# The first mixture of experts routed in blocks of 64 slots instead of run densely, and a reordered front in the last mixture

## The chip, the cores and the metric

One core of a Trainium2 chip runs the whole program. The metric is the device time of one execution in microseconds (us). Engines: TensorE (PE; its weight loads are PEld), VectorE (DVE), ScalarE (ACT), GpSimd (POOL) and SyncE (SP), which issues most DMAs. Each engine runs its own instruction list in order, and semaphores order the engines among each other.

## The reference, cut to what matters

A two-layer perceiver block on 512 tokens (8 sequences of 64) of width 256. The change touches the feed-forward part of layer 0, behind its small attention, and a little of the feed-forward part of layer 1:

```python
# layer 0: every token, the two best of 8 experts, hidden width 512
probs = softmax(mla_out @ router_w + router_b)
topw, topi = top_k(probs, 2)
topw = topw / (topw.sum(-1, keepdims=True) + 1e-08)
combine = sum(one_hot(topi, 8) * topw[..., None], axis=-2)
h1 = gelu(einsum('bsd,edf->ebsf', mla_out, w1) + b1)
h2 = einsum('ebsf,efd->ebsd', h1, w2) + b2
return hs + 0.3 * einsum('bse,ebsd->bsd', combine, h2)
# layer 1: the same with the one best of 8 experts, hidden width 1024, silu
```

The reference multiplies every token by every expert and weighs with `combine`, which is zero for six of the eight.

## The kernel before, in words

The program is a row of stages, each a block that all engines enter and leave together (the branch that ends a block is named by its line; "PEq" as a releaser is this barrier). `core.x` (in the trace: resid) is the residual, 512 tokens as 4 tiles of 128 x 256. PSUM has eight banks of 128 x 512 fp32.

**Layer 0's mixture, `Mixture` with `Gate` and `Experts` (tiles d_*).** It is dense. Its input is c_mlaT (128 x 2 x 512, features on partitions), which ACT writes at the end of the attention block in `ffn0`. TensorE computes router logits (L966), DVE the softmax, ranks and weights (L929 to L952). For each of 8 experts TensorE then computes 4 hidden chunks of 128 features for all 512 tokens (`first`) and 4 x 4 output tiles (`second`). Each product of two fp32 matrices is made as three fp32r matmuls of a high and a low part (`product3`, L186). ACT and POOL split the weights into these parts (L1068, L1041), ACT applies Gelu (L1084) and splits h (L1088), DVE takes its low part (L1107) and adds each expert's output, times the token's weight, to x (L1115). Expert loops are `each`: first and last iteration written out, a hardware loop between. b2 is added once for all experts by the matmul of transposed weights (L1194). Four of the weight splits (`experts.high`, `gpsimd_first`) stand in the attention block ahead, on ACT (L1068 at 259 to 271 us) and POOL.

**Layer 1's mixture, `Routed` (tiles k_*).** It is routed already, with one choice a token. 8 + 7 = 15 blocks of 64 slots hold the tokens sorted by expert; a pair of blocks fills 128 slots. The order of the work on each engine is written out by hand. TensorE counts the tokens before each one (L2640), DVE turns this into a slot number a token (L2542 to L2553), then a 0/1 matrix (`gather_map`, L2570) with which TensorE gathers 256 slots a time (`gather`, L2663) into PSUM, and DVE copies them to k_xg (`gathered`, L2560). Groups 0 and 1 of slots are gathered so; groups 2 and 3 come by device memory: POOL scatters the normalised rows with an indirect DMA (L2466), reads them back in slot order (L2470), and TensorE transposes them (`gather_rows`, L2673). A pair's step is `hidden` (L2689: fp32, 64 slots a matmul, the two blocks of a pair in the two 64-column halves of the array), activation, `turn` (L2701), a copy of the transposed h on ACT (L2498), and `output` (L2718). Results of pairs below VIA go to device memory (L2474) and come back by token with four indirect DMAs (L2479); the last two pairs go back through matmuls with 0/1 matrices (`scatter`, L2728). Experts of blocks 8 to 14 depend on the data: SP reads their numbers from k_expert (`value_load`, L2449) and loads their weights. `warm` (L96) is a run of matmuls whose result nobody reads. TensorE adds b2 ahead of the first gather (L2653), and DVE writes `gather_map(1)` ahead of `gathered(0)`.

## Time and profile before

| | us |
|---|---|
| three executions | 1010.16, 1007.88, 1010.75; median 1010.16 |
| the profiled execution | 1008.23 |
| its span, first to last instruction | 1006.5 |
| mean granted TensorE clock | 0.984 |
| TensorE matmuls busy | 962.3 (96%) |
| weight loads / DVE / ACT / POOL busy | 798.6 / 552.5 / 498.2 / 180.8 |

Times of rows are us from the span's start. A timeline row gives start, duration, engine, line, operation, output<-input, the count of merged instructions, and in brackets how long the engine sat idle before it and what released it. One fp32 matmul shows as two records, a transpose or fp32r matmul as one.

### The profile page before, as it was taken

Reading aid. Unit: us, or ns where it says so; the run is one execution under the profiler, and the core shown is the slowest. Engines: PE = TensorE matmul, PEld = TensorE weight load, DVE = VectorE, ACT = ScalarE, POOL = GpSimd, SP = SyncE. Lnnn points to the kernel's source line nnn. Section 1 sums busy time; section 2 is a strip of 40 time slices with the busy share of each in tenths; the row PEclk is TensorE's granted clock in tenths of the full one; section 3 lists DMA queues with packets and bytes.
Section 4 is the critical chain, followed back from the end, with each engine's and each line's share of the span. In section 5 each row is a group of like instructions: output and inputs, shape, how many; then the busy total and the mean of one; then the engine's idle time right before and its main releaser. Section 6 shows DMA issues by size and latency. Waiting matters only on the chain. (4 is left out here: it accounts for less than half of the span.)

```text
span 1006.5 us, 20977 instructions
## 1 busy us (share of the span) xinstructions
PE 962.3 (96%) x8756; PEld 798.6 (79%) x8756; DVE 552.5 (55%) x800; ACT 498.2 (49%) x716; POOL 180.8 (18%) x188
## 2 busy tenths in 40 slices
PE   8999999888899999899999999999999999998997
PEld 7888887665689985689999999998989996656554
DVE  5677777666443354655646465656464642367222
ACT  5777776353666645454444454454444532321332
POOL 2000000022224423022221222222222101420101
PEclk9999999899999999999999999999999999997999
DMA  5111110022022304111111111111113000599895
GB/s 172 69 47 48 47 49 3 3 62 65 12 81 89 93 20 167 43 42 43 43 43 42 42 42 42 42 42 42 42 62 136 0 1 1 138 327 306 283 346 185
DMA packets 57365, 84.55 MB, mean 84 GB/s; under 512 B 5505, under 2 KB 46162, under 8 KB 57298
## 3 DMA queue, kind: packets, MB, share of 16 engines
q1 hardware_dynamic: 56466, 81.22, 25.6%
q0 software_dynamic: 832, 2.36, 0.7%
q8 instruction: 52, 0.85, 0.3%
q14 instruction: 15, 0.12, 0.0%
HBM read 80.94 MB, written 2.62 MB: 83 GB/s over the span
## 5 line engine op out<-in xcount | busy, mean ns | idle before, releaser
L186 PE MATMUL ps<-f_pT_hi,f_cN_hi 128*128 128x256 f32 x512 | 145.4, 284 | 0.0
L186 PE MATMUL ps<-f_pT_hi,f_cN_lo 128*128 128x256 f32 x512 | 144.7, 283 | 0.0
L186 PE MATMUL ps<-f_pT_lo,f_cN_hi 128*128 128x256 f32 x512 | 144.7, 283 | 0.0
L1596 ACT ACTIVATE e_pr<-ps,e_negmax 128x1024 f32<-128x1024 f32 x64 | 71.5, 1117 | 129.9 <-DVE e_negmax L1601 127.6
L1870 DVE TENSOR_TENSOR f_pT_lo<-ps,f_pT_hi 128x1024 fp32r<-128x1024 f32 x64 | 78.3, 1224 | 81.8 <-ACT f_pT_hi L1808 81.7
L186 PE MATMUL ps<-e_cT_hi,e_qb_hi 128*128 128x512 f32 (+1 forms) x288 | 115.3, 400 | 0.0
L186 PE MATMUL ps<-e_cT_hi,e_qb_lo 128*128 128x512 f32 (+1 forms) x288 | 109.8, 381 | 0.0
L186 PE MATMUL ps<-e_cT_lo,e_qb_hi 128*128 128x512 f32 (+1 forms) x288 | 109.1, 379 | 0.0
L1808 ACT CAST f_pT_hi<-ps 128x1024 fp32r<-128x1024 f32 x64 | 64.9, 1014 | 84.6 <-PE ps L1920 83.8
L445 DVE SCALAR_TENSOR_TENSOR a_u<-ps,a_floor,a_cap 128x1024 f32<-128x1024 f32 x64 | 79.2, 1279 | 48.2 <-PE ps L540 47.7
L186 PEld LDWEIGHTS ps<-f_pT_hi,f_cN_hi 128*128 128x128 f32 x512 | 97.8, 191 | 2.6 <-issue 0.8
L186 PEld LDWEIGHTS ps<-f_pT_lo,f_cN_hi 128*128 128x128 f32 x512 | 97.9, 191 | 1.7
L186 PEld LDWEIGHTS ps<-f_pT_hi,f_cN_lo 128*128 128x128 f32 x512 | 97.9, 191 | 0.0
L356 ACT ACTIVATE a_pr<-a_u,a_nb 128x1024 f32<-128x1024 f32 x64 | 73.8, 1152 | 43.7 <-DVE a_u L445 42.4
L1601 DVE TENSOR_REDUCE e_negmax<-ps 128x1 f32<-128x1024 f32 x64 | 78.1, 1221 | 31.0 <-PE ps L186 30.7
L1591 POOL TENSOR_TENSOR e_cT_lo<-e_raw,e_cT_hi 128x512 fp32r<-128x512 f32 x32 | 40.3, 1292 | 160.7 <-ACT e_cT_hi L1790 160.7
L1920 PE MATMUL ps<-ident,e_pr 128*128 128x128 f32 x512 | 66.3, 272 | 2.5 <-PEq L1625 1.2
L1774 POOL TENSOR_TENSOR f_cN_lo<-e_raw,f_cN_hi 128x512 fp32r<-128x512 f32 x32 | 40.3, 1286 | 141.4 <-ACT f_cN_hi L1797 141.4
L186 PEld LDWEIGHTS ps<-e_cT_hi,e_qb_hi 128*128 128x128 f32 x288 | 54.5, 189 | 11.4 <-issue 1.8
L186 PEld LDWEIGHTS ps<-e_cT_hi,e_qb_lo 128*128 128x128 f32 x288 | 54.3, 188 | 11.2
L1920 PEld LDWEIGHTS ps<-ident,e_pr 128*128 128x128 f32 x512 | 57.8, 140 | 5.5 <-issue 2.8
L186 PEld LDWEIGHTS ps<-e_cT_lo,e_qb_hi 128*128 128x128 f32 x288 | 54.7, 190 | 8.5
(401 smaller groups left out, 1961.8 us busy)
## 6 DMA issues: line engine op xcount, KB each, us to landing
k_w<-in_L_ffn_W SPq DMA_DIRECT2D x30, 1024.0 KB, 13.5
a_ctxT<-in_ctxT SPq DMA_DIRECT2D x16, 512.0 KB, 4.4
d_w<-in_L_ffn_w SPq DMA_DIRECT2D x32, 256.0 KB, 2.7
e_raw<-in_ctxT SPq DMA_DIRECT2D x8, 1024.0 KB, 4.9
e_raw<-in_ctx SPq DMA_DIRECT2D x8, 1024.0 KB, 5.5
k_b<-in_L_ffn_b SPq DMA_DIRECT2D x14, 256.0 KB, 12.0
k_w<-in_L_xattn_w_q SPq DMA_DIRECT2D x1, 1024.0 KB, 5.0
e_wk<-in_L_xattn_w_k SPq DMA_DIRECT2D x1, 1024.0 KB, 7.5
```

What stands on the lines that cost most here:

```text
L186: last = nc.tensor.matmul(out, a[i], b[j], start=start and n == 0, stop=stop and n == 2, skip_group_check=skip)
L356: A.activation(pr[:, n % NP, :], u[:, n % NU, :], ACT.Square, bias=nb[:], scale=HD ** -0.5).then_inc(p_ready, 1)
L445: V.scalar_tensor_tensor(u[:, n % NU, :].rearrange("p (r w) -> p r w", r=RT), core.psum[:, 0:2048].rearrange("p (r w) -> p r w", r=RT)[:, ...
L1591: nc.gpsimd.tensor_tensor(cT[1][:, c, cols], rawT[:, c, cols], cT[0][:, c, cols].bitcast(F32), ALU.subtract).then_inc(t_lo, 1)
L1596: nc.scalar.activation(pr[:, p % NPR, :], core.ps[p % 2][:], ACT.Exp, bias=negmax[:, p:p + 1], accum_out=total[:, p:p + 1]).then_inc(exp_r ...
L1601: nc.vector.tensor_reduce(negmax[:, p:p + 1], core.ps[p % 2][:], AX, ALU.max, negate=True).then_inc(max_ready, 1)
L1774: nc.gpsimd.tensor_tensor(cN[1][:, ks, :], raw[:, ks, :], cN[0][:, ks, :].bitcast(F32), ALU.subtract).then_inc(n_lo, 1)
L1808: nc.scalar.copy(pT[0][:, g, :, P * (p % 2):P * (p % 2) + P], core.ps[2][:].rearrange("p (k n) -> p k n", n=P)).then_inc(pT_hi, 1)
L1870: nc.vector.tensor_tensor(pT[1][:, g, :, cols], core.ps[2][:].rearrange("p (k n) -> p k n", n=P), pT[0][:, g, :, cols].bitcast(F32), ALU.s ...
L1920: last = nc.tensor.transpose(core.ps[2][:, k * P:(k + 1) * P], pr[:, p % NPR, k * P:(k + 1) * P], core.ident[:])
```

## The change

**Layer 0's mixture.** `Gate`, `Experts` and `Mixture` go; `Paired` takes their place. Two choices a token make 1024 places in 8 + 15 = 23 blocks of 64 slots, that is 12 pairs in 6 groups of 256 slots. Products are plain fp32, nothing is split except the gather's input. The weights of blocks 0 to 7 (1 MB an expert) are all loaded in the attention block ahead, into 8 of 14 ring places; those of the 15 data-dependent blocks follow in the mixture. Groups 0 to 2 are gathered by matmul, 3 to 5 by device memory; pairs 0 to 8 return by device memory, in two gathers a token tile, and pairs 9 to 11 by fp32 matmuls with a matrix that holds the token's weight. The four weight splits in the attention block go, on ACT and POOL alike. Two DMAs fill the unused rows with zeros.

```diff
+class Paired:
+    RING = 14
+    BS = 64
+    TOP = 2
+    LAST = 3
+    ROWS_FROM = 3
...
+        self.EXTRA = (self.TOP * NT - 1) // self.BS
+        self.NB = E + self.EXTRA
+        self.NP = (self.NB + 1) // 2
+        self.NG = self.NP // 2
...
+    def prepare_sync(self, sp):
...
+        for e in range(E):
+            self.load(sp, e, e)
+        sp.wait_ge(self.zeroed, 1)
+        for rows, first in ((self.x_rows, 2 * P * self.ROWS_FROM), (self.y_rows, P * (self.NP - self.LAST))):
+            n = self.NP - first // P
+            sp.dma_start(rows[first:, :].rearrange("(i p) d -> p i d", p=P), bc(self.zero[:], 1, n)
+                         ).then_inc(self.zero_out, 16)
...
+            @block.sync
+            def _(sp):
+                sp.wait_ge(expert_ready, 1)
+                for i in range(EXTRA):
+                    k = E + i
+                    if k >= RING:
+                        sp.wait_ge(y_psum, (k - RING) // 2 + 1)
+                    self.load(sp, k, sp.value_load(expert[0:1, i:i + 1], min_val=0, max_val=E - 1))
+            @block.gpsimd
+            def _(pool):
...
+                for i in range(2):
+                    for j in range(TT):
+                        g.indirect_dma_start(self.x_rows, rows(i, j), mrows[:, j, :], None).then_inc(x_put, 16)
+                pool.wait_ge(x_put, 16 * 2 * TT)
+                for i in range(NG - RF):
...
+                for n in range(VIA):
+                    pool.wait_ge(y_copied, n + 1)
+                    g.dma_start(self.y_rows[P * n:P * n + P, :], whole[n % 2][:]).then_inc(y_out[n % 2], 16)
+                pool.wait_ge(y_out[0], 16 * ((VIA + 1) // 2))
+                pool.wait_ge(y_out[1], 16 * (VIA // 2))
+                for j in range(TT):
+                    for i in range(2):
+                        g.indirect_dma_start(back[i][:, j, :], None, self.y_rows, rows(i, j)).then_inc(y_back[j], 16)
+            @block.scalar
+            def _(act):
...
+                for i in range(4):
+                    rows(i)
+                for q in range(NG):
+                    if q >= 1:
+                        taken(2 * q - 2)
+                        taken(2 * q - 1)
+                    if 2 * (2 * q + 1) + 1 >= E and not chosen:
+                        act.wait_ge(expert_ready, 1)
+                        chosen += [act.value_load(expert[0:1, i:i + 1], min_val=0, max_val=E - 1) for i in range(EXTRA)]
+                    turned(2 * q)
+                    turned(2 * q + 1)
+                taken(NP - 2)
+                taken(NP - 1)
...
+                for q in range(NG):
+                    if q >= 1:
+                        hidden(2 * q)
+                        output(2 * q - 2)
+                        hidden(2 * q + 1)
+                        output(2 * q - 1)
+                    turn(2 * q)
+                    turn(2 * q + 1)
+                    if 2 * q - 1 >= VIA:
+                        scatter(2 * q - 1)
+                    if q + 1 < NG:
+                        (gather if q + 1 < RF else gather_rows)(q + 1)
+                output(NP - 2)
+                scatter(NP - 2)
+                output(NP - 1)
+                scatter(NP - 1)
```

`turned(n)` is eight Gelu activations of 128 x 64 (four feature chunks, two blocks of a pair, each with its expert's bias); `taken(n)` copies a pair's output out of PSUM; `scatter_map` and `spread` build the weighted matrices.

**Layer 1's mixture.** The b2 matmuls move behind the last `output`, eight more warming matmuls stand at their old place, and `gathered(0)` moves ahead of `gather_map(1)`.

```diff
+                gathered(0)
                 gather_map(1)
-                gathered(0)
...
-                core.warm(2, 1)
-                pe.wait_ge(mineT_ready, 1)
-                pe.wait_ge(self.b_in, 16)
-                for j in range(TT):
-                    t.matmul(acc(j), mineT[:, j * P:(j + 1) * P], self.b2[:], start=j % 2 == 0, stop=False,
-                             skip_group_check=True)
+                core.warm(2, 9)
...
                 for n in steps(NP - 1):
                     output(n)
+                pe.wait_ge(mineT_ready, 1)
+                pe.wait_ge(self.b_in, 16)
+                for j in range(TT):
+                    t.matmul(acc(j), mineT[:, j * P:(j + 1) * P], self.b2[:], start=False, stop=False,
+                             skip_group_check=True)
                 scatter(NP - 1)
```

**The order of instructions.** First, ACT in the new mixture, from the table load of the first `turned` on; d_hT rows are the Gelu activations, d_whole rows are `taken`, and L1104 is the `value_load` line:

```order
169 L1082 ACT_TABLE_LOAD
170 L1082 ACTIVATE d_hT<-ps,d_b 128x64 x16
171 L1094 COPY d_whole<-ps 128x256 x2
172 L1082 ACTIVATE d_hT<-ps,d_b 128x64 x16
173 L1094 COPY d_whole<-ps 128x256 x2
174 L1104 TENSOR_LOAD d_expert
175 L1104 ISA x2
176 L1104 TENSOR_LOAD d_expert
177 L1104 ISA x2
```

Fifteen such TENSOR_LOADs with their two register instructions stand between `taken(3)` and the activations of pair 4. The dense mixture had none on any engine.

Second, TensorE in the new mixture around the join of two rounds (L1303 hidden, L1324 output, L1314 turn, L1281 gather_rows; the rows are consecutive from the last output matmuls of pair 3 on):

```order
828 L1324 MATMUL ps<-d_w_6,d_hT 64x256
829 L1324 MATMUL ps<-d_w_7,d_hT 64x256
830 L1314 MATMUL ps<-ident,d_h 128x128 x8
831 L1281 MATMUL ps<-ident,d_xr 128x128 x4
832 L1303 MATMUL ps<-d_w_12,d_xg 64x512
833 L1303 MATMUL ps<-d_w_13,d_xg 64x512
834 L1303 MATMUL ps<-d_w_12,d_xg 64x512
835 L1303 MATMUL ps<-d_w_13,d_xg 64x512
836 L1324 MATMUL ps<-d_w_8,d_hT 64x256
837 L1324 MATMUL ps<-d_w_9,d_hT 64x256
```

The gather of a group stands directly ahead of the hidden layer that reads it, and only one hidden layer stands between the transposes of pair 4 and its output.

Third, the end of the program on TensorE, before:

```order
2310 L2718 MATMUL ps<-k_w_6,k_hT 64x256 x8
2311 L2728 MATMUL ps<-k_y_hi,k_permT 128x256
2312 L2728 MATMUL ps<-k_y_lo,k_permT 128x256
2313 L2728 MATMUL ps<-k_y_hi,k_permT 128x256
2314 L2728 MATMUL ps<-k_y_lo,k_permT 128x256
```

and now:

```order
2288 L2827 MATMUL ps<-k_w_6,k_hT 64x256 x8
2289 L2867 MATMUL ps<-k_b,k_mineT 128x256 x4
2290 L2837 MATMUL ps<-k_y_hi,k_permT 128x256
2291 L2837 MATMUL ps<-k_y_lo,k_permT 128x256
2292 L2837 MATMUL ps<-k_y_hi,k_permT 128x256
```

The four b2 matmuls now stand between the last output and the last scatter.

## Rows read from the trace of the kernel before

**Rows 1.** The page: busy time of each engine.

```profile
PE 962.3 (96%) x8756; PEld 798.6 (79%) x8756; DVE 552.5 (55%) x800; ACT 498.2 (49%) x716; POOL 180.8 (18%) x188
```

**Rows 2.** Windows: us, busy (count) PE, PEld, DVE, ACT, POOL, PE clock, DMA share, GB/s.

```profile
274.00:278.00 4.00, 3.17 (x16) 3.10 (x16) 1.51 (x3) 1.11 (x2) 0.00 (x0) 0.60 0.54 162
...
283.00:373.00 90.00, 89.33 (x570) 80.43 (x569) 36.23 (x62) 57.88 (x93) 36.16 (x28) 1.00 0.24 70
...
917.00:919.00 2.00, 2.00 (x11) 1.88 (x10) 1.14 (x4) 0.00 (x0) 0.00 (x0) 0.50 0.99 260
...
925.00:933.00 8.00, 8.00 (x28) 6.55 (x28) 5.72 (x29) 0.26 (x1) 3.20 (x4) 0.50 1.08 315
...
934.00:999.60 65.60, 64.94 (x454) 35.84 (x452) 13.75 (x21) 22.02 (x39) 8.70 (x12) 1.00 0.88 289
```

**Rows 3.** Timeline, where layer 0's mixture begins.

```profile
271.93 0.38 ACT L1361 ACTIVATE c_aoT<-ps,c_bv 128x128 f32<-128x128 f32 x1
...
274.37 3.17 PE L966 MATMUL ps<-d_gate_w,c_mlaT 128*128 128x8 f32 x16 [0.82 <-PEq L1275]
...
278.35 0.23 ACT L959 ACTIVATE d_gate_p<-d_gate_p 128x32 f32<-128x32 f32 x1 [2.96 <-DVE d_gate_p L931]
...
281.11 0.42 DVE L944 TENSOR_REDUCE d_gate_rank<-d_gate_gt 128x32 f32<-128x256 f32 x1
```

**Rows 4.** Timeline, where it ends and the next block begins.

```profile
375.31 0.74 DVE L1142 BATCH_NORM_STATS2 stats<-resid 128x6 f32<-128x256 f32 x2
...
376.59 2.25 PE L96 MATMUL ps<-ident 128*128 128x128 f32 x18 [1.53 <-PEq L1224]
```

**Rows 5.** Timeline, two pairs' steps in layer 1's mixture.

```profile
964.19 1.09 PE L2701 MATMUL ps<-ident,k_h 128*128 128x128 f32 x8
...
972.25 1.09 PE L2701 MATMUL ps<-ident,k_h 128*128 128x128 f32 x8
...
973.18 0.60 PE L2673 MATMUL ps<-ident,k_xr 128*128 128x128 f32 x4
...
973.71 3.65 PE L2689 MATMUL ps<-k_w,k_xg 128*64 128x512 f32 x16
```

**Rows 6.** Timeline, the front of layer 1's mixture.

```profile
924.17 0.22 DVE L2542 TENSOR_TENSOR k_more<-ps,k_steps 128x56 f32<-128x56 f32 x1 [0.70 <-PE ps L2643]
...
925.31 3.78 PE L2653 MATMUL ps<-k_b,k_mineT 8*128 8x256 f32 x8
...
926.58 1.14 DVE L2570 TENSOR_SCALAR k_perm<-k_slots,k_slot 128x256 fp32r<-128x256 f32 x4
927.63 0.86 DVE L2575 TENSOR_SCALAR k_diag<-ident,k_slot 128x128 f32<-128x128 f32 x4
...
929.02 0.58 PE L2663 MATMUL ps<-k_perm,k_x_hi 128*128 128x256 f32 x1
...
932.60 1.51 PE L2737 MATMUL ps<-k_diag,k_ones 128*128 128x128 f32 x8
932.84 0.69 DVE L2560 COPY k_xg<-ps 128x512 f32<-128x512 f32 x1 [1.83 <-PE ps L2663]
```

**Rows 7.** One line, SP's value_load: duration ns min/median/max, first and last start.

```profile
L2449 SPq TENSOR_LOAD <-k_expert x7: 263/442/482, 929.2 to 933.2; - x7
L2449 SPq FUSED_REGOPS  x7: 147/147/173, 929.7 to 933.7; - x7
```

**Rows 8.** Timeline, the end of the program.

```profile
989.59 0.54 POOL L2474 DMA_DIRECT2D k_y_rows<-xnT  x1 [7.52 <-ACT xnT L2505]
...
994.76 1.02 POOL L2479 DMA_INDIRECT xn<-k_y_rows,k_place  x1 [4.63 <-issue]
...
998.61 0.95 POOL L2479 DMA_INDIRECT xn<-k_y_rows,k_place  x1 [0.30 <-issue]
...
1000.61 0.36 PE L2728 MATMUL ps<-k_y_hi,k_permT 128*128 128x256 f32 x1 [1.02 <-DVE k_y_lo L2604]
```

**Rows 9.** One line, ACT's weight splits: columns as in rows 7.

```profile
L1068 ACT CAST d_w_hi<-d_w x32: 609/618/625, 259.3 to 363.0; 128x512 fp32r<-128x512 f32 x32
```

More of the change, by code:

```diff
@@ L1201 @@
[L1201 to L1224 removed]
+                        pattern=[[1, P]], channel_multiplier=-1).then_inc(self.const, 1)
@@ new lines, in _ @@
+                for i in range(2):
+                    step(V.reduce_sum(wts[i][:], pick[i][:], AX), i == 1)
+                for i, values in enumerate((slot[0], slot[1], wts[0], wts[1])):
+                    spread(i, values)
+                gather_map(1)
+                for q in range(NG):
+                    copied(2 * q)
+                    copied(2 * q + 1)
+                    if q + 1 < NG:
+                        gathered(q + 1)
+                    if q + 2 < RF:
+                        gather_map(q + 2)
+                    if q == 2:
+                        dve.wait_ge(row_ready, 4)
+                        for n in range(VIA, NP):
+                            scatter_map(n)
@@ new lines, in scatter @@
+                def scatter(n):
+                    pe.wait_ge(map_ready, n - VIA + 1)
+                    pe.wait_ge(y_copied, n + 1)
+                    for j in range(TT):
+                        last = t.matmul(acc(j), back_to[n - VIA][:, j * P:(j + 1) * P], whole[n % 2][:],
+                                        start=False, stop=n == NP - 1, skip_group_check=True)
+                    last.then_inc(placed, 1)
+                pe.wait_ge(m_lo, 1)
+                gather(0)
+                hidden(0)
@@ new lines, in _ @@
+                hidden(1)
+                pe.wait_ge(weighed, 1)
+                for j in range(TT):
+                    last = t.transpose(y_bank[0:E, j * P:(j + 1) * P], wt[:, j, :], core.ident[:])
+                last.then_inc(wT_psum, 1)
+                for i in range(4):
+                    spread(i)
+                pe.wait_ge(wT_ready, 1)
+                pe.wait_ge(self.b_in, 32)
+                for j in range(TT):
+                    t.matmul(acc(j), wT[:, j * P:(j + 1) * P], self.b2[:], start=j % 2 == 0, stop=False,
+                             skip_group_check=True)
@@ L1528, in _ @@
                 output(1)
-        mixture.run(mlaT, None, finished)
+        mixture.run(mlaT)
 def xattn1(core, a, finished, early):
```

623 lines of the change are left out of this document (332 added, 291 removed).

## The prediction

> **What bounds the kernel now.** I read the page first: TensorE's matmuls are busy for 96% of the span [rows 1], so before each stage's waits are looked at, its TensorE time counts. The windows then show the stage that changes: from 283 to 373 us TensorE is busy for 89.33 of 90.00 us at clock 1.00 (the 2.4 GHz level), while DVE, ACT and POOL have slack [rows 2]. The dense mixture is bound by matmuls alone. The timeline gives its ends: router logits start at 274.37 us [rows 3], the next block's first matmul at 376.59 us [rows 4]. So the stage takes 102.2 us, and this is what the routed version must beat. I count from L, the start of the logits.
>
> Layer 1's mixture is the model for the new one, since the instructions have the same shapes. One step there (hidden, output, turn) for a half pair takes 4.03 us: the transposes of two pairs start at 964.19 and 972.25 us with two steps between [rows 5]. In 65.6 us it makes 15 such steps at clock 1.00 [rows 2].
>
> **The change part by part.** What goes is some 90 us of full TensorE work. What comes is 12 pair steps of 4.03 us, 48.4 us, as each pair of 64-slot blocks has one 512-wide hidden chunk. Three matmul gathers add about 2.0 us each at the full level (the one of 929.02 to 932.60 us took 3.6 us at clock 0.50 [rows 2, 6]), three `gather_rows` 0.60 us each [rows 5], three scatters 1.7 us each (four 256-column fp32 matmuls of 0.43 us: 512 columns for each block pair take 3.65/8 = 0.46 us in two concurrent halves [rows 5], twice that alone). All this is 61 us. The rest is waits, since work is now in short pieces that pass from engine to engine.
>
> *Front, L to L+19.4.* Logits 3.2 us [rows 3]; eight transposes at the half level, L+5.1; ACT then makes two copies of about 1.05 us, L+7.3, and DVE the low part, 1.2 us, plus waits, L+9.0. Ranks are ready sooner (281.5 us, L+7.2 [rows 3]), so the warming matmuls ahead of the counts are not late. DVE's slot chain took 2.4 us in layer 1 (924.17 to 926.58 us [rows 6]); it is longer by some two-choice operations, 2.8 us: L+11.9. `gather_map(0)` is 4 operations as before (1.14 us [rows 6]) and 4 with two inputs of about 0.45 us: 3.0 us, L+14.9. TensorE has then waited some 3 us, and I take the gather at the half level, as in layer 1, 3.6 us; the copy to d_xg with its hand-overs (932.60 to 933.5 us there, 0.9 us [rows 6]) ends at L+19.4.
>
> *To the first `turn`, L+37.5.* `hidden(0)` and `hidden(1)`: 3.65 us at the full level [rows 5], 1.5 us more for the part at the half level, L+24.6. Weight transposes, 0.6 us. Then four `spread`s follow each other: DVE's four diagonals (0.86 us), TensorE's eight records (1.51 us at clock 0.5, half of that else) [rows 6], ACT's copy beside DVE. I take 2.35 us a turn, L+34.6, with the level falling meanwhile. `gather_map(1)` stands behind the last diagonals on DVE and ahead of `copied(0)`, which `turn(0)` waits for: 3.0 us and two copies of 0.7 us give L+37.5. The b2 matmuls (3.78 us at the half level [rows 6]) run beside this.
>
> *Rounds.* Two turns and `gather(1)` partly at the half level, 4.1 us, copy 0.9 us: L+42.5. A round is 8.06 us plus its gather, and since the gather stands right ahead of `hidden` the 0.9 us copy is waited for in each: in layer 1 another hidden layer hid it. Round 1 takes 11.0 us (L+53.5), round 2, whose gather is the short one, 9.6 us (L+63.1). One `turned` is eight activations. A 32-column one without a bias row takes 0.23 us, a 128-column one with bias 0.38 us [rows 3]; between them, less overlap, I take 0.27 us each, 2.2 us, and it fits under `gather` and `hidden`.
>
> *The fifteen loads.* In round 2 ACT reads 15 expert numbers right after `taken(3)`, which ends about L+60.6. No ACT row shows such a load. The nearest are SP's seven: starts from 929.2 to 933.2 us, 0.67 us apart, made of 0.44 us for the load and 0.15 us for its register operation [rows 7]. Fifteen are 10.0 us; with the shortest load (0.26 us) and almost nothing else the lower bound is 4.8 us, and with the longest ones and gaps the upper 11 us. I take 10.0: L+70.6, activations 2.2 us, L+72.9. TensorE could go on at L+64.9 (`hidden(6)` done), so it stands for 8.0 us. After such a pause it starts at 1.2 GHz. In layer 1's front the 8.0 us from 925 us ran at clock 0.50 without a gap before the level rose [rows 2]; I charge 7 us at half speed, 3.5 us lost. Without the pause both terms go. The Trainium skill, DMA: Bandwidth & Descriptors, section "Latency and other measured facts", puts a `tensor_load` floor at about 600 ns and says that the compiler unrolls four times "to amortize". The trace disagrees on the floor: its median is 442 ns [rows 7]. By the page's floor with SP's register time the fifteen would cost 11.5 us; what its amortizing would give is the first rival below.
>
> *To the end.* The rest of round 3 is 9.7 us with the lost time, its gather 1.5 us: L+84.1; round 4, L+93.7. In round 5 pair 8 is out of PSUM 4.2 us later, L+97.9. Its rows must be in memory before the gathers back: from POOL's last write to its first indirect gather 5.2 us passed [rows 8]. Then eight gathers of 1.28 us follow on POOL (four from 994.76 to 998.61 us started that far apart [rows 8]), where layer 1 has four: L+113.3. Landing 1.7 us (estimate from the end of that trace), two additions 0.95 us, then four additions of the matmul part and four statistics, 3.2 us, barrier 0.5 us: L+119.7. TensorE's own path (three scatters between the last outputs) would be done at L+111.7, so POOL's gathers end the stage. The stage is 17.5 us longer than 102.2.
>
> *Around it.* In the attention block ahead four ACT splits of 0.62 us go [rows 9], which stood between exponentials and copies: gain between 0 and 2.5 us, I take 1.1. The 8 MB of early weights flow while TensorE runs small tiles; the mixture's last six ring places and nine reloads have 20 us or more of slack each at 289 GB/s [rows 2], so nothing is charged. Behind the stage TensorE has now stood still before the barrier; after such a gap the stretch from 917 us ran at 0.50 [rows 2]: 1.4 us lost, between 0 and 3.
>
> *Layer 1's front.* Nine warming matmuls at the half level take 9 x 0.43 = 3.8 us, as long as one and the b2 matmuls of 3.78 us [rows 6] less 0.5 us, so the gather starts 0.5 us sooner; `gathered(0)` waits for TensorE in either order. At the end b2 takes 2 us at the full level where 1.02 us was idle [rows 8]. I take zero, between 1.2 us gained and 0.6 us lost.
>
> The sum: 17.5 - 1.1 + 1.4 + 0 = 17.8 us on the profiled execution's 1008.23 us, **1026 us**. That execution is 1.9 us below the median of the runs shown, which widens the range a little and moves nothing else. About 0.3% is what a measurement of this kernel can tell from no change.
>
> **Rivals.**
> *The loads are amortized* or run beside ACT's waits. For it: only a register is written, and SP's first load took 0.26 us. Against: each of SP's seven was followed by its register operation at an even pace [rows 7]. Below about 1.7 us for all fifteen TensorE hardly waits; the 8.0 us pause shrinks to 0 or 1 and its 3.5 us go: 1015 us. This is the page's amortizing carried out. By spreads and tail at their better ends, 1008.
>
> *The waits hide, not slower.* TensorE's work decides, as before the change: front to L+19.4, then 12 steps, gathers, scatters and spreads back to back, about 65 us, and 4 us behind them, L+88.6, 13.6 us shorter: 995 us. It takes TensorE work between `hidden(1)` and `turn(0)`, under each copy and under the loads. It decides from the point where less than some 13 us of the waits remain; I count about 30. Against it stands the written order, which leaves nothing to run in those places.
>
> *The half level stays.* TensorE works in pieces of 2 to 8 us with gaps of 0.9 us; if the level does not rise again in rounds 3 and 4, two rounds cost 8 us more each in the worst case, about 10 together: 1036 us. Against: layer 1's steps hold 1.00 [rows 2], though with fewer gaps.
>
> **How the numbers follow.** Forecast 0.55, loads amortized 0.22, waits hidden 0.10, half level 0.13. The forecast's own range is 1017 to 1034: loads 5.2 us less, spreads and tail 2 to 4 us either way, around it 2 us. Ten per cent below go with hidden waits and the best amortized cases; some below the top with the last rival: 1010 to 1037. Faster by over 0.3%: 0.08, nearly all from hidden waits. Within 0.3%: 0.10, from the better half of the amortized case. Slower: 0.82.
>
> **What would show it.** Right: 15 loads in ACT's queue at 0.6 to 0.7 us, TensorE idle before `output(4)` for about 8 us with a clock near 0.5 behind it; about 37 us from logits to `turn(0)`; POOL's eight indirect gathers as the last thing that DVE waits for; rounds of 9.6 us. Wrong: loads below 0.3 us, TensorE at 1.00 through the stage, spreads that overlap with `hidden`, a weight that TensorE waits for, or a stage of under 100 us.

## The result, and the profile after

| | before | after |
|---|---|---|
| median of the runs, us | 1010.45 (1007.88 to 1012.66) | 1024.72 (1020.29 to 1029.0) |
| the profiled execution, its span | 1008.23, 1006.5 | 1029.0, 1027.3 |
| mean granted clock | 0.984 | 0.972 |
| TensorE busy | 962.3 | 955.7 |
| layer 0's mixture, logits to the next block | 102.2 | 117.4 |

The ratio is 1.0147, 95% interval [1.0118, 1.0175]: slower, near the forecast of 1026.0. TensorE is busy for 6.6 us less in all (in the new mixture for 90.1 us where the dense one had 99.1) and yet the span is 20.8 us longer. From the starts of four stages, the difference of the spans splits as follows: up to layer 0's logits -0.3 us, the new mixture +15.2, all between it and layer 1's logits +1.8, from there to the end +4.1. That sums to 20.8.

First the page of the changed kernel, to be held against [rows 1]:

```profile
span 1027.3 us, 20845 instructions
PE 955.7 (93%) x8718; PEld 769.4 (75%) x8718; DVE 554.0 (54%) x837; ACT 467.1 (45%) x733; POOL 165.0 (16%) x195
```

TensorE in the new mixture, from the timeline of the changed kernel (the first and last rows answer to the logits of [rows 3] and to the next block of [rows 4]). L1303 is `hidden`, L1290 `spread`, L1349 b2, L1314 `turn`, L1324 `output`, L1332 `scatter`:

```profile
274.06 1.92 PE L1244 MATMUL ps<-d_gate_w,c_mlaT 128*128 128x8 f32 x16 [0.82 <-PEq L1389]
290.55 5.67 PE L1303 MATMUL ps<-d_w,d_xg 128*64 128x512 f32 x16 [0.79 <-DVE d_xg L1169]
296.58 1.06 PE L1290 MATMUL ps<-d_diag,d_ones 128*128 128x128 f32 x8
299.07 1.16 PE L1290 MATMUL ps<-d_diag,d_ones 128*128 128x128 f32 x8 [1.43 <-issue]
303.34 2.08 PE L1290 MATMUL ps<-d_diag,d_ones 128*128 128x128 f32 x8 [3.11 <-DVE d_diag L1181]
...
312.09 1.97 PE L1314 MATMUL ps<-ident,d_h 128*128 128x128 f32 x8
317.26 1.94 PE L1303 MATMUL ps<-d_w,d_xg 128*64 128x512 f32 x8 [0.78 <-DVE d_xg L1169]
...
337.44 1.94 PE L1303 MATMUL ps<-d_w,d_xg 128*64 128x512 f32 x8 [0.78 <-DVE d_xg L1169]
345.78 3.64 PE L1324 MATMUL ps<-d_w,d_hT 128*64 128x256 f32 x16 [6.40 <-ACT d_hT L1082]
355.11 1.94 PE L1303 MATMUL ps<-d_w,d_xg 128*64 128x512 f32 x8 [0.78 <-DVE d_xg L1169]
...
372.43 1.89 PE L1332 MATMUL ps<-d_whole,d_map 128*128 128x256 f32 x8
380.16 3.56 PE L1332 MATMUL ps<-d_whole,d_map 128*128 128x256 f32 x8 [3.96 <-issue]
391.50 2.25 PE L96 MATMUL ps<-ident 128*128 128x128 f32 x18 [2.27 <-PEq L975]
```

The brackets are the waits. I cut the stage in three: the **front** from the logits to `hidden(2)` (317.26), 43.2 us; the **rounds** to the first `scatter` (372.43), 55.2 us; the **tail** to the next block, 19.1 us. These three numbers are the yardstick for every experiment below.

The same stage in windows, with the granted clock before the DMA share (compare [rows 2], where TensorE was busy without a gap at 1.00):

```profile
core 0: us, PE busy (x) PEld busy (x) DVE busy (x) ACT busy (x) POOL busy (x), PEclk, DMA share, GB/s
290.00:293.00 3.00, 2.45 (x6) 0.77 (x8) 2.72 (x16) 0.00 (x0) 1.75 (x2) 0.50 0.94 317
...
317.00:337.00 20.00, 18.61 (x132) 10.81 (x132) 6.60 (x15) 4.89 (x20) 2.22 (x4) 1.00 0.72 250
337.00:345.00 8.00, 1.94 (x8) 0.48 (x8) 7.21 (x11) 1.02 (x6) 0.00 (x0) 0.84 1.07 371
345.00:349.00 4.00, 3.22 (x16) 1.89 (x18) 0.00 (x0) 2.37 (x12) 0.00 (x0) 0.50 0.72 244
349.00:372.00 23.00, 21.43 (x153) 11.42 (x150) 4.84 (x7) 9.02 (x38) 3.62 (x6) 0.99 0.21 76
```

In the rounds TensorE is busy for 93% of its time at the full level, except in one hole of 6.4 us, behind which the level is 0.50 for 4 us. The hole is ScalarE's: between its copy of pair 3 and pair 4's Gelu activations, with nothing but the 15 register loads (ScalarE's queue at their line, columns as in [rows 7]: shortest, median and longest ns):

```profile
L1104 ACTq TENSOR_LOAD <-d_expert x15: 272/275/483, 335.3 to 343.3; - x15
L1104 ACTq FUSED_REGOPS  x15: 147/147/168, 335.8 to 343.6; - x15
L1104 ACTq SEQ_ASSERT  x15: 18/18/29, 336.0 to 343.8; - x15
```

```profile
343.98 3.39 ACT L1082 ACTIVATE d_hT<-ps,d_b 128x64 f32<-128x64 f32 x16 [8.36 <-issue]
```

The loads start 0.57 us apart on the mean (8.0 us between the first and the last, 14 steps). The first load is the longest (0.48 us), the next is as long as the last (0.28 and 0.27 us), so there is no saving that grows along the row.

### The profile page after: what moved, and what is told of

Read it like the earlier page. It is cut to its first block and busy times, and to the rows that moved or that the text cites. A ratio compares the mean times of both kernels' runs of the same rounds, so it can differ in the third digit from the quotient of the medians.

```text
span 1027.3 us, 20845 instructions
## 1 busy us (share of the span) xinstructions
PE 955.7 (93%) x8718; PEld 769.4 (75%) x8718; DVE 554.0 (54%) x837; ACT 467.1 (45%) x733; POOL 165.0 (16%) x195
## 3 DMA queue, kind: packets, MB, share of 16 engines
q1 hardware_dynamic: 67346, 98.13, 29.8%
## 5 line engine op out<-in xcount | busy, mean ns | idle before, releaser
L186 PE MATMUL ps<-e_cT_hi,e_qb_hi 128*128 128x512 f32 (+1 forms) x288 | 115.5, 401 | 0.0
L1922 ACT CAST f_pT_hi<-ps 128x1024 fp32r<-128x1024 f32 x64 | 65.1, 1018 | 84.6 <-PE ps L2034 84.1
L186 PEld LDWEIGHTS ps<-e_cT_hi,e_qb_hi 128*128 128x128 f32 x288 | 54.5, 189 | 11.5 <-issue 1.8
```

What stands on the lines that cost most here:

```text
L186: last = nc.tensor.matmul(out, a[i], b[j], start=start and n == 0, stop=stop and n == 2, skip_group_check=skip)
L1922: nc.scalar.copy(pT[0][:, g, :, P * (p % 2):P * (p % 2) + P], core.ps[2][:].rearrange("p (k n) -> p k n", n=P)).then_inc(pT_hi, 1)
```

## The experiments

The experiments ran on three chips, here A (**again**, **loads_early**, **last_alone**, **warm_more**), B (**first_alone**, **gather_sooner**, **rows_later**, **joined**) and C (**again_more**, **before_again**, **loads_gather**, **joined_mended**). A ratio is against runs of the kernel before on the same chip. All stage lengths come from timelines of TensorE, one profiled execution each, cut as above:

| | ratio, interval | front | rounds | tail | stage | layer 1's logits to end |
|---|---|---|---|---|---|---|
| before | 1 | | | | 102.2 | 86.4 |
| before_again (C) | 0.9986 [0.9976, 0.9997] | | | | 100.8 | 88.7 |
| after | 1.0147 [1.0118, 1.0175] | 43.2 | 55.2 | 19.1 | 117.4 | 90.5 |
| again (A) | 1.0086 [1.0059, 1.0112] | 35.9 | 56.3 | 14.7 | 106.9 | 90.1 |
| again_more (C) | 1.0132 [1.0112, 1.0151] | 40.6 | 55.6 | 19.3 | 115.5 | 90.0 |
| loads_early (A) | 0.9997 [0.997, 1.0024] | 39.3 | 47.0 | 14.7 | 100.9 | 90.5 |
| warm_more (A) | 1.0051 [1.0029, 1.0073] | 36.1 | 56.0 | 14.6 | 106.7 | 89.0 |
| last_alone (A) | 0.9997 [0.9975, 1.0019] | | | | 102.3 | 85.7 |
| first_alone (B) | 1.0075 [1.0047, 1.0104] | 41.8 | 56.0 | 14.7 | 112.5 | 87.5 |
| gather_sooner (B) | 1.0084 [1.0057, 1.011] | 36.9 | 55.2 | 14.7 | 106.8 | 89.4 |
| rows_later (B) | 1.0057 [1.0029, 1.0085] | 29.4 | 62.7 | 14.7 | 106.8 | 89.8 |
| joined (B) | 0.9972 [0.9952, 0.9992] | 32.5 | 51.8 | 14.8 | 99.0 | 88.9 |
| loads_gather (C) | 1.0053 [1.0033, 1.0073] | 46.0 | 44.7 | 20.1 | 110.8 | 90.5 |
| joined_mended (C) | 1.001 [0.9993, 1.0026] | 28.6 | 55.4 | 19.3 | 103.2 | 92.8 |

Two warnings on this table. The stretch between layer 0's mixture and layer 1's logits is the same program in all fourteen traces, and yet it took from 541.1 us (**joined_mended**) to 547.0 (**joined**); the span of a single trace can't be read more finely than that. And part of a front's length is settled before anything that an experiment moved (but for the added warming matmuls): the first hidden group, `hidden(0)` with `hidden(1)`, started 15.7 us (**joined_mended**) to 19.2 us (**first_alone**, **loads_early**) behind the logits, by the level at which what stands ahead of it ran. So where it matters I also give the stage from that group's start on: 90.8 us in **again**.

### The changed kernel again

No edit.

> The changed kernel once more, unaltered. In its profile TensorE's results came late twice without a releaser: 3.4 us behind the second spread (299 to 302.4 us) and 3.6 us behind output(10) (376 to 379.6 us). If these belong to one execution, this profile has them elsewhere or not at all and the stage takes 111 to 114 us in place of 117.4. If they belong to the program, they stand in the same places and the stage takes 117 us again.

1018.31 us (4 runs). Its span is 1015.6 us, 11.7 less than the first trace, and the stage, 106.9 us, is shorter than either case had it. The rounds differ by 1.1 us; the front is 7.3 us shorter and the tail 4.4. TensorE's rows of that second trace:

```profile
294.92 1.06 PE L1290 MATMUL ps<-d_diag,d_ones 128*128 128x128 f32 x8
296.96 1.16 PE L1290 MATMUL ps<-d_diag,d_ones 128*128 128x128 f32 x8 [0.98 <-DVE d_diag L1181]
299.09 1.16 PE L1290 MATMUL ps<-d_diag,d_ones 128*128 128x128 f32 x8 [0.97 <-DVE d_diag L1181]
...
304.64 1.97 PE L1314 MATMUL ps<-ident,d_h 128*128 128x128 f32 x8
339.52 3.68 PE L1324 MATMUL ps<-d_w,d_hT 128*64 128x256 f32 x16 [6.62 <-ACT d_hT L1082]
371.40 1.97 PE L1332 MATMUL ps<-d_whole,d_map 128*128 128x256 f32 x8 [0.56 <-ACT d_whole L1094]
```

The waits of 3.11 and 3.96 us are not in it. The pause ahead of `output(4)` is. So the pause belongs to the kernel, the other two to an execution or a chip; **again_more** comes back to them.

### The register loads

```diff
                 A.copy(mrows[:], tokens).then_inc(m_rows, 1)
+                act.wait_ge(expert_ready, 1)
+                chosen += [act.value_load(...) for i in range(EXTRA)]
...
-                    if 2 * (2 * q + 1) + 1 >= E and not chosen:
-                        act.wait_ge(expert_ready, 1)
-                        chosen += [act.value_load(...) for i in range(EXTRA)]
```

> The 15 expert numbers are read on ACT right after the copy of the gather's input, where ACT is idle until about 296.7 us. My theory: the pause ahead of output(4) (6.4 us in the profile) and the half level behind it (1.7 us) go, nothing takes their place, the stage is 7 to 9 us shorter and the program takes about 1017 us. Rival, a hidden cover: the weights of pair 4 or POOL's reads take the place of the loads, and less than 3 us are gained.

1011.52 us against 1018.31 on the same chip: 6.8 us gone, and the kernel is level with the one before. The loads themselves are nearly as long as they were, only elsewhere (the queue rows of **loads_early**):

```profile
L1066 ACTq TENSOR_LOAD <-d_expert x15: 273/275/483, 290.6 to 298.2; - x15
```

ScalarE has nothing else to do there: its next step, the copy of the transposed weights, waits for TensorE until 298.81 us. TensorE's wait for `d_hT` is gone from the list of waits, and the rounds fall from 56.3 to 47.0 us: 9.3 us, which is the pause of 6.6 us, 1.8 us that `output(4)` took longer (3.68 for 1.90), and 0.9 us that the next matmuls did. Of this the front gave back 3.3 us in this execution, so the stage is 5.9 us shorter and not the 7 to 9 expected. That was the clock, not the edit: the logits took 2.58 us here and 2.05 in **again**, the warming matmuls ahead of the counts 4.62 and 3.52, and the first gather 3.7 us and 2.1; all three began ahead of the first of the moved loads (290.6 us, the gather at 289.96). From the first hidden group on the stage took 81.8 us against 90.8, 9.0 us less.

### Layer 1's edit alone

The kernel before, with layer 1's part of the diff only.

> The kernel before with the change of layer 1's mixture alone (b2 behind the last output, nine warming matmuls, gathered(0) sooner). My theory: the first gather starts 0.5 us sooner, the last scatter ends about 1 us later, and the sum is within 1 us of zero. Rival: the front's gain stays and the program is 1.2 us shorter or more; with 3 rounds only the rows of the profile can tell these apart.

0.9997 [0.9975, 1.0019], no difference to be measured. Its first gather started 4.83 us behind the counts instead of 5.41, as expected, and the stage lengths are those of before within 0.7 us. So the edit in layer 1 is neutral to some 2 us, and the cost comes with the routed first mixture.

### More warming matmuls

```diff
-                core.warm(0, 12)
+                core.warm(0, 26)
```

> 26 warming matmuls in place of 12 behind the counts, which fills TensorE's idle time ahead of gather(0). If the idle time is what takes the clock down, gather(0) and hidden(0), hidden(1) run at the full level: 2.0 and 3.65 us in place of 2.7 and 5.67 us, 2.5 to 3 us less up to the end of hidden(1). If the clock falls anyway, or the spreads' chain on DVE hides it, turn(0) does not come sooner.

1015.13 us, 3.2 less than **again**, but the intervals of the two ratios overlap. In the profiled execution TensorE has no wait ahead of the gather any more, and the gather ran at the full level; but it had done so in **again** too, behind a wait of 2.80 us, so this pair of traces differs by 0.1 us in the stage. The row of **warm_more**, then that of **again**, both over the warming matmuls and the time up to the gather:

```profile
280.00:286.00 6.00, 6.00 (x66) 1.00 0.00 0
```

```profile
282.00:288.00 6.00, 3.20 (x40) 1.00 0.00 0
```

Whether the gain is that fewer executions drop to the half level is a guess that two traces can't settle.

### Layer 0's part alone

Layer 1's part of the diff taken back.

> The changed kernel with layer 1's edit taken back: layer 0's mixture stays routed. The run of layer 1's edit alone showed 85.7 us from layer 1's logits to the end (the kernel before: 86.4), but every kernel that routes layer 0's mixture as well shows 89.0 to 90.5: 0.9 us and 2.9 us of TensorE's idle time ahead of its last two matmul groups, with the last weight load issued 62.5 to 63.9 us after the logits instead of 60.7, and the half level after it. Theory A (the 3.7 to 4.1 us come from what the routed layer 0 leaves behind, for instance a DMA stream that lags by 1.5 to 2 us, whatever layer 1's front does): this kernel keeps them, logits to end 89.5 to 91, total within 1.5 us of the changed kernel, ratio to before 1.007 to 1.011. Theory B (it is the two edits together): logits to end 86 to 87, total 3.5 to 4.5 us under the changed kernel, ratio 1.003 to 1.006.

The total goes with theory A: 1.0075, in its range, but this trace's front makes it of little use for that. The stretch that the theories spoke of is 87.5 us, between both. TensorE's wait for the weights of its last hidden group (`<-issue`, the transfer isn't named) was 1.6 us here, 2.6 to 3.6 with both edits. This trace shows a third kind of front: no stall, but the first gather and hidden group at the half level.

```profile
293.57 6.12 PE L1303 MATMUL ps<-d_w,d_xg 128*64 128x512 f32 x16 [0.78 <-DVE d_xg L1169]
```

Those 16 records took 3.66 us in **again**, and the front is 5.9 us longer.

### The gather ahead of the last output

```diff
                         hidden(2 * q + 1)
+                    if q + 1 < NG:
+                        (gather if q + 1 < RF else gather_rows)(q + 1)
+                    if q >= 1:
                         output(2 * q - 1)
                     turn(2 * q)
...
-                    if q + 1 < NG:
-                        (gather if q + 1 < RF else gather_rows)(q + 1)
```

> In each round TensorE gathers the next pair of blocks ahead of the last output group instead of behind both turns, so that VectorE's copy of the gathered rows (0.69 us, six waits of 0.78 us, 4.7 us in all in the trace of the changed kernel) runs beside a matmul group. Theory A (each wait is on the path of the end): the six waits shrink to under 1 us together and the stage is 3.5 to 4.5 us shorter, ratio to before 1.003 to 1.007 where the unchanged kernel has 1.0086. Theory B (the waits are slack, since the weights' transfers or ScalarE's 15 register loads set the time): the pause of 6.4 to 6.6 us ahead of block 4's output grows by as much as the waits shrink in the first two rounds (some 1.6 us), and at most 2 to 3 us are gained.

1.0084: nothing gained in the total. The list of TensorE's waits in this stage shows why:

```profile
PE ps L1324 <- ACT d_hT L1082: 7.8, 1, 7.8
...
PE ps L1303 <- DVE d_xg L1169: 0.8, 1, 0.8
```

Five of six waits for VectorE's copy are gone, 3.9 us. The pause ahead of `output(4)` grew by 1.2 us, as theory B had it, and the rounds are only 1.0 us shorter than in **again**. The front is 0.9 us longer, but not by the edit: the first hidden group started 17.4 us behind the logits instead of 16.0, since the warming matmuls (4.42 us for 3.52) and the first gather ahead of it ran slower. From that group on the stage took 89.4 us against 90.8. So the move gave 1.4 us; theory A is out for this kernel (the ratio is outside its range, too) and theory B holds.

### The spreads in round 1

```diff
-                for i in range(4):
-                    spread(i)
...
                         hidden(2 * q)
+                        if q == 1:
+                            spread(0)
                         output(2 * q - 2)
+                        if q == 1:
+                            spread(1)
                         hidden(2 * q + 1)
...
```

The copies on ScalarE and the diagonals on VectorE move with them, and the spreads use the gather's PSUM bank.

> The four spreads of the tokens' slots and weights along the free axis (four times 8 matmuls, two VectorE and one ScalarE step each, between the first hidden group and the first turn) are taken out of the front and done in the first round, between its matmul groups. In the changed kernel they take 7.4 us at the full level and 11.9 us at the half one, with 1 us of waiting before each of three. Theory A (the front's length is on the path of the end): the first turn is 7 to 12 us sooner after the logits (29.8 us in the repeated run), some 4 to 5 us of TensorE work come back in round 1, and the stage is 3 to 6 us shorter; ratio to before 1.003 to 1.006. Theory B (the time is set by the weights' transfers, which start at the same moment whatever the front does): the first turn is sooner by as much, but hidden groups later wait for weights, and under 1 us is gained.

The first `turn` came 23.2 us after the logits instead of 29.8, and the front is 6.6 us shorter. The rounds are 6.5 us longer. The ratio lies in theory A's range, but its interval overlaps with that of **again**, and the stage, 106.8 us, is no shorter (90.8 us from the first hidden group on, as there). Both mechanisms fail: nothing waited for weights, and TensorE's four groups of 1.16 us with a new wait cost in round 1 what they had cost in the front. The waits of **rows_later**:

```profile
PE ps L1336 <- ACT d_hT L1082: 6.4, 1, 6.4
PE ps L1317 <- DVE d_xg L1174: 4.7, 6, 0.8
...
PE ps L1304 <- DVE d_diag L1186: 1.6, 1, 1.6
```

### All moves joined

The three moves above (loads, gather, spreads), with 26 warming matmuls, and layer 1's part of the diff taken back. In round 1 the gather stands behind `output(1)`, the last spread and `turn(2)`.

> All moves at once: the 15 register loads on ScalarE directly behind the copy of the tokens' counts, spreads in round 1, gather ahead of the last output of each round, 26 warming matmuls behind the counts instead of 12, layer 1's edit taken back. If the terms add (loads 7 to 8 us, spreads 3 to 6, gather 3 to 4, warming 0 to 3, layer 1 0 to 4, from 1.0086 of before): 13 to 20 us under the changed kernel, ratio to before 0.989 to 0.996, that is faster than both. If the weights' transfers become the bound of the stage (8 MB more than nothing: the stage's DMA share was over 0.9 where the engine had no pause): TensorE's waits for k or d weights appear, and the ratio stops at 0.996 to 1.000.

1008.39 us, 0.9972 [0.9952, 0.9992] of before, and 9.4 us under **first_alone** on the same chip; the sum of the terms, 13 us at least, was not reached, and no wait for weights took its place in this stage. The pause and most waits are gone. What took their place stands in its list of waits:

```profile
PE ps L1358 <- ACT d_wT L1068: 2.6, 1, 2.6
PE ps L1303 <- DVE d_diag L1185: 1.6, 1, 1.6
PE ps L1316 <- DVE d_xg L1173: 1.1, 2, 0.8
PE ps L1343 <- ACT d_whole L1096: 1.1, 2, 0.6
```

The first is new: the 15 loads now keep ScalarE from its copy of the transposed weights.

How much of this is more than the loads alone? From the first hidden group on the stage took 81.3 us, against 81.8 in **loads_early**. So the gather and the spreads added 0.5 us to what moving the loads gave, and the two ratios, 0.9972 and 0.9997, have overlapping intervals: a gain of the further moves isn't shown.

### Chip C: the changed kernel, the kernel before, and two combinations

> The changed kernel once more, unchanged, for a second pair of traces. Two profiled executions of it differ by 11.7 us in their spans (1027.3 and 1015.6): 8.2 us lie ahead of the first turn (L+38.0 and L+29.8, L being the start of the first mixture's logits), where one ran its first hidden group and its spreads at the half level (5.67 us and 2.08 us for what took 3.66 and 1.16 in the other). Theory A (the level that the clock has in the front differs from execution to execution and makes the spread of the times): the first turn comes at 29.5 to 30.5 or at 35 to 38 us, and the stage's length follows it: 106 to 108 us in the first case, 112 to 115 in the second; ratio to before 1.007 to 1.012. Theory B (the first trace was a disturbed one, the rest is constant): the first turn at 29.5 to 30.5, the stage 106.5 to 107.2, ratio 1.0075 to 1.0095.

1.0132, first `turn` 34.8 us after the logits, stage 115.5. Theory B is out. Theory A has the lengths nearly right (the ratio is above its range) but the cause wrong: the hidden group ran at the full level (3.66 us), and then TensorE stalled. TensorE's rows in **again_more**:

```profile
295.73 1.16 PE L1290 MATMUL ps<-d_diag,d_ones 128*128 128x128 f32 x8 [0.97 <-DVE d_diag L1181]
299.72 2.08 PE L1290 MATMUL ps<-d_diag,d_ones 128*128 128x128 f32 x8 [2.83 <-issue]
...
371.63 1.95 PE L1324 MATMUL ps<-d_w,d_hT 128*64 128x256 f32 x16
377.69 3.65 PE L1332 MATMUL ps<-d_whole,d_map 128*128 128x256 f32 x8 [4.11 <-issue]
```

and ScalarE's beside them:

```profile
298.79 0.58 ACT L1071 COPY d_row<-ps 128x512 f32<-128x512 f32 x1 [3.35 <-remote]
377.17 0.37 ACT L1094 COPY d_whole<-ps 128x256 f32<-128x256 f32 x1 [4.12 <-remote]
```

The output group shows an end at 373.58 us; ScalarE, which had nothing to do but copy it, began at 377.17. In **again** TensorE waited 0.56 us for the same hand-over. VectorE's diagonals were released at 298.79 us too, in the same moment as ScalarE's copy. After each of these two stalls the level is 0.50, and the next matmuls take nearly twice their time. The waits of the first trace (1.43, 3.11 and 3.96 us) look the same. All three traces of chip C with a routed first mixture have a stall in the front and this one in the tail; the seven traces of such kernels on chips A and B have neither, nor has **before_again** on chip C. In **again_more** both stalls fell while GpSimd issued its indirect DMAs, 1.25 to 1.27 us apart and without a gap; it did so in the traces without a stall, too.

> The kernel before, profiled a second time, as the control for layer 1's stage: its logits to the end took 86.4 us in the first trace, 85.7 with layer 1's edit alone, 87.5 with the routed first mixture alone, and 88.9 to 90.5 in the six traces with the routed mixture and TensorE's waits for the last weights (0.2 and 1.3 us without the routed first mixture, 1.6 to 3.8 with it). Theory A (the routed first mixture makes it longer): 85.7 to 86.6 again, waits for weights under 1.3 us. Theory B (the lateness of the weights differs by 3 us from execution to execution whatever the first mixture does): 87.5 or more is as likely as not. Ratio to before 0.998 to 1.002 in both.

The kernel before on chip C: 0.9986, no stall, stage 100.8 us, and 88.7 us for layer 1's part, with this wait for the last weights:

```profile
990.11 1.94 PE L2689 MATMUL ps<-k_w,k_xg 128*64 128x512 f32 x8 [1.26 <-issue]
```

Part of theory B holds: an unchanged kernel differs by 2.3 us in this stretch from one execution to the next. Of the 3.6 to 4.1 us that the comparison of the changed kernel with the first trace gave to layer 1, 1.3 to 1.8 are left against this one. The waits themselves, 0.2, 1.3 and 1.3 us without the routed first mixture and 1.6 to 3.6 in eleven traces with it, still speak for a small effect. Its cause stays open: transfers fill the DMA engines there in all kernels (a share of about 1 from 30 to 70 us behind the logits), and over the first 70 us before, **last_alone** and the changed kernel moved the same amount, 22.2 to 22.5 MB by the windows.

> The gather ahead of each round's last output, together with ScalarE's register loads behind its copy of the counts. Alone the gather's move took out 3.9 of the 4.7 us of waits for VectorE's copy, yet the stage stayed at 106.8 us: the pause ahead of output(4) grew from 6.6 to 7.8 us, and the first two rounds ran later by 1.0 us. Theory A (the register loads' pause swallowed it, since those loads wait for ScalarE's own work and not for TensorE): without the pause the move is worth 2.5 to 4 us, the stage 97 to 98.5 us against 100.9 with the loads early alone, ratio to before 0.993 to 0.998 (the loads early alone: 0.9997). Theory B (other waits take the place, weights above all): the stage 100 to 101 us, ratio 0.999 to 1.001.

1.0053. The total says little, since the profiled execution had three stalls (3.6 and 3.1 us at the spreads, 4.1 in the tail), and front and tail are the longest of all. The rounds can be read: 44.7 us, 2.3 less than with the loads early alone (47.0), where the same move had given 1.0 us of 56.3 with the pause in place. So the pause had swallowed somewhat over half of the move, and theory A is right in kind and high in size: five waits of 0.78 us are 3.9 us, of which 2.3 come back.

> The joined kernel with the 15 register loads one step later on ScalarE: behind its copy of the weights' transpose, where it waits 7.8 us for the first turn anyway, instead of ahead of it, where they made TensorE wait 2.6 us. Theory A (that wait is on the path): the wait is gone, the loads end within 0.5 us of the first turn, the stage is 1.5 to 2.6 us shorter than the joined kernel's 99.0, ratio to before 0.994 to 0.996 (joined: 0.9972). Theory B (the loads now end behind the first turn and push ScalarE's first gelu group out by as much): under 0.5 us is gained, ratio 0.997.

1.001 [0.9993, 1.0026]: no gain over **joined**. TensorE's wait for the transposed weights fell from 2.6 to 0.7 us; in its place there are 3.1 us for the gathered rows, 2.0 us for the first activations and 4.1 us in the tail:

```profile
PE ps L1316 <- DVE d_xg L1173: 4.2, 3, 3.1
PE ps L1343 <- issue: 4.1, 1, 4.1
...
PE ps L1335 <- ACT d_hT L1084: 2.0, 1, 2.0
```

Theory A's condition isn't met: the loads took 10.5 us instead of some 8.4, by a stall, and ended 6.0 us behind the first `turn`; without the stall it would be about 4 us (estimate from these two numbers), since the first `turn` now comes 24.5 us behind the logits and not 31.5. What the move is worth by itself can't be told from this trace: the stalls lie over it, and layer 1's stretch, 92.8 us, was 3.9 us longer than in **joined** with the same wait for weights of 3.0 us, because more of it ran at the half level (granted clock 0.55 in its first 15.2 us, 0.64 in **joined**'s first 14.4; the hidden group behind the wait 3.68 us for 1.94).

The stall of chip C fell into the loads this time, and so it can be looked into. ScalarE's queue at the line of the loads, from 299 to 301 us:

```profile
L1068 ACTq FUSED_REGOPS  x2: 705/706/706, 298.4 to 299.8; - x2
L1068 ACTq SEQ_ASSERT  x1: 689/689/689, 299.1 to 299.1; - x1
```

Elsewhere these take 147 and 18 ns. Register instructions that wait for no engine took 0.7 us each, VectorE's copy, for which the gather had been done at 298.2, began at 301.42, and SP's next weight load at 301.19. So this stall held ScalarE, VectorE and SP together, and is no matter of TensorE's signal alone; GpSimd's indirect writes went on 1.26 us apart. What causes it was not found.

The joined moves are worth 9.4 us against **first_alone** on chip B and, in this form, 11.0 us against **again_more** on chip C. They bring the routed mixture level with the dense one (0.9972 and 1.001), not clearly under it, and the loads alone had done nearly as much.

## Why the prediction was right, point by point

The sign and the main cause were right: TensorE was busy for less time, and waited in a chain of small hand-overs with one big hole. The size was right in part by luck: the total of 1026 was met with the help of two things that weren't in it, the stalls with the half level around them (10.6 us of the stage, against **again**) and 4.1 us in layer 1's mixture. On chip A, with no stall, the same sum comes to +9.1 us of span, not +17.8; the median there, 1018.31, is still inside the range of 1017 to 1034. Step by step, L being the start of the logits, with the first trace and **again**:

| step | predicted | first trace | again |
|---|---|---|---|
| first hidden group starts | L+19.4 | L+16.5 | L+16.0 |
| first `turn` | L+37.5 | L+38.0 | L+29.8 |
| front, to `hidden(2)` | 42.5 | 43.2 | 35.9 |
| round 1, round 2 | 11.0, 9.6 | 10.8, 9.4 | 10.8, 9.4 |
| round 3 with the pause | 21.0 | 17.7 | 18.8 |
| round 4 | 9.6 | 9.4 | 9.4 |
| `hidden(10)` to the next block | 26.0 | 27.0 | 22.6 |
| stage against before | +17.5 | +15.2 | +4.6 |

- **Front.** Mis-sized by 6.6 us where no stall fell on it. I took the logits at 3.2 us from the one row there was, where they took 1.9 to 3.2 in these traces, and charged the half level to gather, hidden and the logits together. The four spreads came 2.1 us apart in **again**, 2.35 predicted. VectorE's maps took 2.9 us, as predicted, but ran beside the last spread's matmuls and copy instead of behind them, and `turn(0)` came 1.7 us behind that copy. In the first trace 2.6 us of stalls and the half level around them filled all this up.
- **Rounds.** 11.0 and 9.6 us were right within 0.3. The wait for the copy of the gathered rows was there each time, 0.78 us for the 0.9 taken. The activations were over-priced: sixteen take 3.39 us, 1.7 us for one `turned` instead of 2.2.
- **The loads.** Right in place and kind: 15 in ScalarE's queue, TensorE idle ahead of `output(4)`, half level behind. Sizes: 0.57 and 0.59 us apart instead of 0.67, 8.4 us in all instead of 10.0; pause 6.4 instead of 8.0; 1.8 to 2.7 us at the half level instead of 3.5. Together 8.2 to 9.3 us for the predicted 11.5, and **loads_early** took 9.3 out of the rounds. SP's median of 0.44 us [rows 7] was the wrong row to go by; SP's own loads in the new mixture have a median of 0.27. I had also read that row wrongly: SP's first load took 0.48 us, its fourth 0.26, and the seven came 0.5 and 0.8 us apart by turns, not at an even pace.
- **Rival, amortized loads.** It fell: the loads have their full length. Its number, 1015, is nearer to chip A's 1018 than the forecast is, for another reason, the front.
- **Rivals, hidden waits and lasting half level.** Neither came. In **again** 21 us of TensorE's waits stood in the stage, more than the 13 from which the first decides; **joined**, which does put work into them, came out level and not 13 us faster. TensorE was at 0.99 to 1.00 in rounds 1, 2 and 4.
- **The tail.** The step that failed in its parts. From the last write of y to the first indirect gather it took 2.3 us, not the 5.2 of [rows 8]. The eight gathers came 1.27 us apart, as predicted, and the last additions for them ended at L+109.8 in the first trace, 4.3 us ahead of the end of TensorE's last scatter. There it was TensorE, with its stall of 3.4 us and a scatter at half speed, that ended the stage, not GpSimd's gathers. In **again** the two ended within 0.7 us of each other, the additions for GpSimd's gathers last. The rows of the first trace (L is 274.06):

```profile
368.84 0.54 POOL L1048 DMA_DIRECT2D d_y_rows<-d_whole  x1 [5.36 <-ACT d_whole L1094]
371.10 1.02 POOL L1053 DMA_INDIRECT xnT<-d_y_rows,d_place  x1 [1.72 <-DMA d_y_rows<-d_whole]
```

```profile
383.36 0.48 DVE L1227 SCALAR_TENSOR_TENSOR resid<-c_mlaT,d_wt,resid 128x256 f32<-128x256 f32 x1
```

```profile
386.15 1.96 PE L1332 MATMUL ps<-d_whole,d_map 128*128 128x256 f32 x8 [0.56 <-ACT d_whole L1094]
```

- **Around it.** Neither term can be read. For the 1.1 us of the attention block ahead: the logits start at 274.06 and 274.88 us, 274.37 before, but at 271.96 to 275.25 in all eleven traces of routed first mixtures and at 274.20 to 275.85 in the three of dense ones. Behind the stage 1.8 and 0.3 us were lost for the predicted 1.4, in a stretch that differs by 5.9 us among traces.
- **Layer 1.** Taken at zero. **last_alone** says zero. In the changed kernel its stretch was 3.6 to 4.1 us longer than in the first trace of before and 1.3 to 1.8 longer than in the second; the gather did start 4.83 us behind the counts instead of 5.41, as predicted, and the time was waited away at the last weights.

The price of a load comes out as follows. The register steps took 0.57 us each with a load of 0.275 us in it. The Trainium skill, DMA: Bandwidth & Descriptors, section "Latency and other measured facts", gives about 600 ns as the floor of one `tensor_load`; the trace has less than half of that for the load, and near that for the whole step. By the same section of the Trainium skill the compiler unrolls four times by default to amortize. These fifteen stand written out one behind the other, and no saving shows: behind the first, longer one each took its full step. Whether another way of unrolling saves anything no run here shows.

## What to carry to other kernels

A routed mixture that trades 99 us of nearly unbroken matmul time for 86 us in short groups (**again**) has to be judged by its hand-overs: here TensorE's waits in the stage rose from 3 to 21 us and ate all of the gain, and one batch of fifteen scalar register loads on an engine of the critical path made most of the loss (6.8 of 8.2 us on chip A). Put such a batch where its engine waits anyway, and look ahead of it for what it then delays. Moving TensorE work out of a front is worth nothing if the place it goes to has no hole, and a wait that you remove ahead of a larger pause only makes the pause longer: take out the largest first.

## What the runs showed of the hardware that was not expected

- Two executions of one kernel differed by 11.7 us in their traces. Stalls account for 6.0 us of it (two in the front, together 2.6, and one of 3.4 in the tail), and the clock at 0.50 ahead of them and behind for most of the rest. Such stalls stood in all three traces of a routed first mixture on one chip of three and in the first trace, in none of seven on the two other chips; inside one, register instructions of 18 and 147 ns took 0.7 us. Their cause stays open.
- The level of TensorE's clock in the same stretch of the same program was 1.00 or 0.50 from execution to execution: one hidden group took 3.66, 5.67 or 6.12 us, though the instructions ahead of it were the same.
- One `value_load` on ScalarE is three instructions in the queue, 0.275 + 0.147 + 0.018 us, and the next follows 0.54 to 0.59 us after it started (means of fifteen), in both places on ScalarE where the batch ran without a stall.
